# A four-direction scan stage, rebuilt: static slots, turned copies in rings, image-wise merge banks and a product on GpSimd

## What is computed

```python
def _s6(x, xw, xb, bcw, bcb, dw, db, yw, yb):
    u = _linear(x, xw, xb)
    bc = _linear(x, bcw, bcb)
    delta = _linear(x, dw, db)
    Bm, Cm = jnp.split(bc, 2, axis=-1)
    A_bar = jnp.exp(-jax.nn.softplus(delta))
    B_bar = (1.0 - A_bar) * Bm
    elems = (A_bar, B_bar * u)
    ...
    _, h = jax.lax.associative_scan(combine, elems, axis=1)
    y = Cm * h
    return _linear(y, yw, yb)
```

## Time and profile before

| | us |
|---|---|
| median of 3 runs (4073.1 to 4082.28) | 4078.38 |
| the profiled execution, its own time | 4069.57 |
| its span, first to last instruction | 4067.7 |
| from the start of the scan stage's first memset to its end in the trace, about | 2589 to 3295 |
| busy over the whole span: TensorE 83%, VectorE 66%, ScalarE 69%, GpSimd 40% | |

### The profile page before, as it was taken

The page is one execution under the profiler, slowest core; times in us unless marked ns, Lnnn a source line. Parts: engine busy times, 40 slices in busy tenths (PEclk is TensorE's granted clock), DMA queues, the critical chain, the costliest instruction groups (busy, mean ns, idle before and its releaser), DMA issues. The chain is left out here.

```text
span 4067.7 us, 72899 instructions
## 1 busy us (share of the span) xinstructions
PE 3375.5 (83%) x20680; PEld 1903.7 (47%) x20680; DVE 2700.0 (66%) x4346; ACT 2799.4 (69%) x5115; POOL 1643.9 (40%) x1502
## 2 busy tenths in 40 slices
PE   5799999978679899999996668699999868677756
PEld 2688888833234344444442224344444324466622
DVE  2566666667059999999999927466666657322256
ACT  4455555568789889898895439577777659566656
POOL 0233333300258889898897610055555510000000
PEclk9899999989889999999999979899999989889989
DMA  4000000012474665757655122100000012400022
GB/s 94 25 14 14 15 14 15 13 49 53 132 193 129 183 189 150 203 142 201 181 148 141 52 70 59 33 16 15 15 15 15 10 32 59 91 17 13 13 55 52
DMA packets 209772, 297.72 MB, mean 73 GB/s; under 512 B 74150, under 2 KB 194134, under 8 KB 209242
## 3 DMA queue, kind: packets, MB, share of 16 engines
q1 hardware_dynamic: 198826, 285.75, 26.9%
q10 hardware_dynamic: 10800, 10.34, 1.1%
HBM read 193.87 MB, written 102.03 MB: 73 GB/s over the span
## 5 line engine op out<-in xcount | busy, mean ns | idle before, releaser
L1586 POOL TENSOR_TENSOR mam_hc<-mam_h,mam_cs 128x896 f32<-128x896 f32 x336 | 703.8, 2095 | 183.8 <-DVE mam_h L1551 86.0
L1551 DVE TENSOR_TENSOR_SCAN mam_h<-mam_a,mam_kept,mam_dbx 128x448 f32<-128x448 f32 x672 | 738.0, 1128 | 23.5 <-ACT mam_a L1437 22.2
L1318 PE MATMUL mam_ps_y<-mam_hc,mam_ident 128*128 128x448 f32 x1344 | 573.3, 560 | 130.6 <-POOL mam_hc L1586 130.4
L1972 POOL TENSOR_TENSOR scan_ch<-scan_h,scan_cs 128x392 f32<-128x392 f32 x256 | 347.4, 1374 | 554.8 <-DVE scan_h L1938 554.8
L1437 ACT ACTIVATE mam_a<-mam_ft,mam_a_neg 128x448 f32<-128x448 f32 x672 | 409.3, 657 | 79.5 <-DVE mam_h L1551 78.6
L1318 PEld LDWEIGHTS mam_ps_y<-mam_hc,mam_ident 128*128 128x128 f32 x1344 | 250.1, 193 | 431.5 <-POOL mam_hc L1586 219.8
L1538 DVE TENSOR_TENSOR mam_dbx<-mam_ps_u,mam_bs 128x448 f32<-128x448 f32 x672 | 381.3, 611 | 32.3 <-DMA mam_bs<-dram_bc 32.3
L766 POOL TENSOR_TENSOR att_prob<-att_prob,att_share 128x588 f32<-128x588 f32 x128 | 151.8, 1186 | 451.6 <-DVE att_share L951 451.6
L1938 DVE TENSOR_TENSOR_SCAN scan_h<-scan_turned_in,scan_start 128x392 f32<-128x392 f32 x192 | 252.8, 1335 | 27.3 <-ACT scan_turned_in L1857 26.0
L1812 PE MATMUL scan_ps_merged<-scan_ch,scan_w_merge 128*128 128x392 f32 x512 | 231.3, 534 | 45.3 <-POOL scan_ch L1972 43.1
L2092 PE MATMUL lstm_ps<-lstm_hs,lstm_w_h 64*128 64x224 f32 x1344 | 171.1, 409 | 97.9 <-DVE lstm_hs L2175 97.9
(11 more groups left out here) (215 smaller groups left out, 7643.4 us busy)
## 6 DMA issues: line engine op xcount, KB each, us to landing
mam_taps<-normed SPq DMA_DIRECT2D x1008, 43.5 KB
mam_bs<-dram_bc SPq DMA_DIRECT2D x28, 896.0 KB, 14.4
mam_cs<-dram_bc SPq DMA_DIRECT2D x28, 896.0 KB, 16.3
mam_ft<-dram_steps SPq DMA_DIRECT2D x42, 448.0 KB, 4.7
normed<-f_staged SPq DMA_DIRECT2D x384, 38.1 KB
f_mixed<-mixed SPq DMA_DIRECT2D x384, 36.8 KB
dram_gs<-mam_gs SPq DMA_DIRECT2D x56, 224.0 KB, 2.3
mam_gt<-dram_gs SPq DMA_DIRECT2D x56, 224.0 KB, 2.7
```

The source lines that it names most:

```text
L1318: mm = pe.matmul(ps_y[p % 2][:, 0:MT], ident[:], hc[t % 2][:, i, :], start=False, stop=(t % 8 == 7 and i == 1))
L1551: dve.tensor_tensor_scan(h[:, n % 8, :], a[t % 3][:, i, :], dbx[:, i, 0:MT], kept[:, at:at + 1], ALU.mult, ALU.add).then_inc(scanned, 1)
L1586: pool.tensor_tensor(hc[t % 2][:], h[:, row:row + 2, :], cs[:, 2 * pair:2 * pair + 2, :], ALU.mult).then_inc(weighed, 1)
L1972: pool.tensor_tensor(out, hd, in_order(cs, 1 - half, d, t, p), ALU.mult).then_inc(weighed, 1)
```

## The change

The stage is written anew with the same split into slots. A pass of the loop now holds a whole stage of eight slots with fixed addresses. The biases of the four projections come in through w_in: a row of ones is loaded once into a spare partition of each image's input tile. Decay is written twice by ScalarE from its PSUM bank, once by row and once turned into a ring `by_column`; drive is turned once per chunk by one copy. Direction 2 is scanned straight from the rings by row, 1 and 3 from the rings by column. The start values are read from the last column of `h`. The products read PSUM directly: ub = U * rest and drive = B * ub. For every direction TensorE makes one 64-row matmul per image with merged and gate side by side in the image's bank, so ScalarE makes the gate in two parts across the halves, and copies the merged values with their bias into `prod`, also in two parts. GpSimd multiplies `prod` by `gate` in place, after its second `ch` of the slot. `ch`, `gate`, `prod`, `result`, `rest` and `ub` have one buffer each. The diff, cut to its core:

```diff
+        by_column = {name: buf.sbuf(f"{name}_by_column", [P, 2 * PIXELS])
+                     for name in ("decay", "drive")}
-        ps_merged = buf.psum("ps_merged", [P, BANK])
-        ps_gate = buf.psum("ps_gate", [P, BANK])
+        ps_merged = [buf.psum(f"ps_merged{image}", [P, BANK]) for image in range(2)]
...
-                with eng.Fori(0, K // 2 - int(peeled)) as t:
-                    for p in range(2):
-                        slot(f, b, half, t + int(peeled), p, b is not None)
+                first = b is not None and isinstance(b, int) and b == 0
+                for k in range(K):
+                    slot(f, b, half, k, k % 2, b is not None and not (first and k == 0))
...
+                for p in range(2):
+                    for image in range(2):
+                        row = 32 * image + C
+                        sp.dma_start(xin[p][row:row + 1], w["ss_ones"]
+                                     ).then_inc(weights_in, 16)
...
             def _(pe):
-                        pe.wait_ge(sided, done(c - 1, 4))
-                        pe.wait_ge(multiplied, done(c - 1))
-                        for i in range(4):
+                        for i, read, count in (
+                                (DELTA, sided, done(c - 1, 4) - 1), (U, multiplied, done(c - 1)),
+                                (C_, sided, done(c - 1, 4)), (B_, fronted, done(c - 1))):
+                            pe.wait_ge(read, count)
                             pe.matmul(ps_in[i][:, 0:N], w_in[:, i, :], xin[p][:, :, 1:SIDE + 1],
                                       start=True, stop=True).then_inc(projected, 1)
...
-                    pe.wait_ge(gated, done(c - 1))
+                    reached(pe, sigmoided, c)
                     for n in range(DIRS):
                         pe.wait_ge(weighed, done(c - 1, DIRS) + (n + 1))
-                        for a, ps in enumerate((ps_merged, ps_gate)):
-                            mm = pe.matmul(ps[:, 0:N], w_merge[:, a, n, :], ch[p][:, n, :],
+                        for rows, ps in zip((IMAGE_0, IMAGE_1), ps_merged):
+                            mm = pe.matmul(ps[:, 0:N], w_merge[rows, n, :], ch[rows, n, :],
                                            start=(n == 0), stop=(n == DIRS - 1))
...
             def _(act):
                 def open_gate(c, p):
                     act.wait_ge(merged, done(c))
-                    act.wait_ge(gated, done(c - 2))
-                    act.activation(gate[p][:], ps_gate[:, 0:N], ACT.Sigmoid,
-                                   bias=merge_b[:, 1:2]).then_inc(sigmoided, 1)
+                    act.wait_ge(gated, done(c - 1))
+                    act.activation(gate[IMAGE_0], ps_merged[0][IMAGE_1, 0:N], ACT.Sigmoid,
+                                   bias=merge_b[IMAGE_1, 1:2])
+                    act.activation(gate[IMAGE_1], ps_merged[1][IMAGE_0, 0:N], ACT.Sigmoid,
+                                   bias=merge_b[IMAGE_0, 1:2])
+                    act.wait_ge(outed, done(c - 1))
+                    for rows, ps in zip((IMAGE_0, IMAGE_1), ps_merged):
+                        op = act.activation(prod[rows], ps[rows, 0:N], ACT.Identity,
+                                            bias=merge_b[rows, 0:1])
+                    op.then_inc(sigmoided, 1)
+                def turn(c, half, k):
+                    act.wait_ge(fronted, done(c))
+                    act.activation(turned_rows("drive", half, k),
+                                   ring(drive, half)[:, k * N:(k + 1) * N].rearrange(
+                                       "p (y x) -> p y x", x=SIDE), ACT.Copy).then_inc(turned, 1)
+                def slot(f, b, half, k, p, has_tail):
+                    if f is not None and k > 0:
+                        turn(f * K + k - 1, half, k - 1)
+                    elif b is not None and k == 0:
+                        turn(b * K + (K - 1), 1 - half, K - 1)
                     if has_tail:
+                        open_gate(b * K + k - 1, 1 - p)
                     if f is not None:
...
+                        act.wait_ge(multiplied, done(c - 1))
                         act.wait_ge(projected, done(c - 1, 4) + 1)
                         act.activation(ring(decay, half)[:, at], ps_in[DELTA][:, 0:N],
+                                       ACT.Sigmoid, scale=-1.0).then_inc(sided, 1)
+                        act.activation(turned_rows("decay", half, k),
+                                       ps_in[DELTA][:, 0:N].rearrange("p (y x) -> p y x", x=SIDE),
+                                       ACT.Sigmoid, scale=-1.0).then_inc(sided, 1)
+                        act.activation(rest[:], ps_in[DELTA][:, 0:N], ACT.Sigmoid
+                                       ).then_inc(sided, 1)
+                        act.wait_ge(projected, done(c - 1, 4) + 3)
+                        act.activation(ring(cs, half)[:, at], ps_in[C_][:, 0:N], ACT.Copy
+                                       ).then_inc(sided, 1)
+                    if has_tail:
+                        store(b * K + k - 1, 1 - p)
...
             def _(dve):
+                def share(f, k, p):
+                    c = f * K + k
+                    dve.wait_ge(sided, done(c - 1, 4) + 3)
+                    dve.wait_ge(projected, done(c - 1, 4) + 2)
+                    dve.tensor_tensor(ub[:], ps_in[U][:, 0:N], rest[:], ALU.mult
+                                      ).then_inc(multiplied, 1)
+                def drive_with(f, half, k, p):
+                    c = f * K + k
+                    dve.wait_ge(multiplied, done(c))
+                    dve.wait_ge(projected, done(c, 4))
+                    dve.tensor_tensor(ring(drive, half)[:, k * N:(k + 1) * N],
+                                      ps_in[B_][:, 0:N], ub[:], ALU.mult
+                                      ).then_inc(fronted, 1)
...
+                def slot(f, b, half, k, p, has_tail):
                     if b is not None:
+                        c = b * K + k
                         dve.wait_ge(fronted, done(b * K + (K - 1)))
                         dve.wait_ge(scanned, done(c - 1, DIRS))
                         dve.wait_ge(weighed, done(c - 2, DIRS))
+                        for n in range(3):
+                            if n == 2:
+                                dve.wait_ge(turned, done(b * K + (K - 1)))
+                            scan(c, 1 - half, k, p, n)
                     if f is not None:
+                        share(f, k, p)               # ub = ps_in[U] * rest
+                    if b is not None:
+                        scan(c, 1 - half, k, p, 3)
+                    if f is not None:
+                        drive_with(f, half, k, p)    # drive = ps_in[B_] * ub
...
             def _(pool):
+                def tail(c, p):
+                    pool.wait_ge(sigmoided, c + 1)
+                    pool.tensor_tensor(prod[:], prod[:], gate[:], ALU.mult).then_inc(gated, 1)
...
-                    pool.wait_ge(merged, done(c - 2))
+                    pool.wait_ge(merged, done(c - 1))
+                    pool.wait_ge(sided, done(b * K + (K - 1), 4))
                     for n, d in enumerate(ORDER):
...
+                        pool.tensor_tensor(out, hd, in_order(cs, 1 - half, d, k), ALU.mult
                                            ).then_inc(weighed, 1)
+                        if n == 1 and has_tail:
+                            tail(c - 1, 1 - p)
```

More of the change, by code:

```diff
@@ L1717, in stage @@
             def stage(f, b, half):
-                peeled = b is not None and isinstance(b, int) and b == 0
-                if peeled:
-                    for p in range(2):
-                        slot(f, b, half, 0, p, p == 1)
-                with eng.Fori(0, K // 2 - int(peeled)) as t:
-                    for p in range(2):
-                        slot(f, b, half, t + int(peeled), p, b is not None)
+                first = b is not None and isinstance(b, int) and b == 0
+                for k in range(K):
+                    slot(f, b, half, k, k % 2, b is not None and not (first and k == 0))
             stage(0, None, 0)
@@ L1837, in store @@
                         act.dma_start(mixed[c + image * (pairs * K)],
[L1838 removed]
+                                      result[32 * image:32 * image + C]).then_inc(left, 16)
                 def tail(c, p):
                     open_gate(c, p)
[L1842 to L1860 removed]
@@ L1876, in slot @@
-                        act.activation(rest[p][:], ps_in[DELTA][:, 0:N], ACT.Sigmoid,
-                                       bias=biases[:, DELTA:DELTA + 1]).then_inc(sided, 1)
-                        act.wait_ge(projected, done(c, 4))
-                        act.activation(ring(cs, half)[:, at], ps_in[C_][:, 0:N], ACT.Identity,
-                                       bias=biases[:, C_:C_ + 1]).then_inc(sided, 1)
+                                       ACT.Sigmoid, scale=-1.0).then_inc(sided, 1)
@@ L1905, in _, with scan @@
                 dve.wait_ge(prepared, 2)
```

(36 more changed lines are left out.)

153 lines of the change are left out of this document (58 added, 95 removed).

## The result

**3977.35 us** is the median of four runs (3973.53 to 3983.29), against 4075.74 for the kernel before (four runs beside them, 4067.93 to 4082.28): a ratio of 0.9761, with a 95% interval of 0.9738 to 0.9783. The profiled execution took 3975.44 us for its span of 3973.6, the one of before 4069.57 us: 94.1 us less.

The account below looks back on a forecast made before the run. A ring of waits set the old slot; GpSimd's chain with collisions the new, 8.6 us. Full slots -81, last slots -8, front-only -6, start +2.5, tail +2: -90.5 from 4078.38, median 3988 us, forecast 3960 to 4015 (0.66), range 3930 to 4045.

Parts of the forecast that it names:

- TensorE, pairs: Merges of a slot become four pairs whose halves run together: TensorE needs 5.9 us a slot, at worst 8.6.
- rival B: Full slots: pairs don't overlap or strided writes cost 1.84 us; slot 9.3 us, total 4028; 0.13 with C's small form.
- GpSimd's chain: From last merge through four ch and the product to the last pair, with scan collisions: 8.64 us a slot.
- ScalarE's road: From last merge over gate and merged parts, decay, rest, ub, fourth scan and ch to merge: 7.83 us before collisions.
- a fourth ch that waits for a scan that waits for ub by more than 1 us: Sign in a slot that the forecast is wrong and ScalarE's road is the bound.
- The turned copies: ScalarE's turned decay and turned drive, written with a stride: 0.92 us each, bounds 0.48 and 1.84.
- The port: Scans with two SBUF inputs and GpSimd multiplications take turns; ub and drive leave it; no slot under 7.8 us.
- The product's own move: Merged times gate goes from VectorE, 0.60 us away from the port, to GpSimd, 1.02 us on it: a loss.
- Start and front-only slots: Stage start: rows of ones add 2.5 us, 0 to 5; front-only slots 4.3 us each, 6 us less, one table load.
- The last eight slots: Slots without a front keep the GpSimd chain: 8.6 us instead of 9.57, 8 us gained.
- Rival C: TensorE's clock falls to 1.2 GHz in part of the slots as waits grow: slower, 4118 us at share 0.6; chance 0.07.
- Rival A: Scans settle into the holes, so the full slot falls to the port's 7.8 us, total 3937; chance 0.10.

## Why the prediction came out right

The number was right by 11 us, and the slot of 8.6 by 0.16. Point by point:

- **TensorE, pairs.** Right: the two halves of a merge pair start within 0.01 us of each other, and the last pair's four passes take 0.93, where I had 0.82. TensorE's busy time fell by 9 of 80 us. The price of losing them was too small, though: rival B gave 0.66 a slot for pairs that don't overlap, the runs 1.44 and 1.35. The step missed that all eight merges queue behind the output product.
- **The bound of the slot.** GpSimd's chain, which I had at 8.64, measures 8.45. Its terms hold: 0.18 to start for 0.20, the product 0.97 for 1.02, a ch by column 1.20 for 1.21, and the collisions together 0.96 in the first two ch and 0.92 before the fourth, 1.88 for 2.09. What I missed is that ScalarE's road, which I had at 7.83 "before any collision", is 8.45 too. Of the difference, 0.59 is the four parts (2.39 instead of 1.80), 0.51 the collision of the fourth scan, which I had left out of this road, and 0.11 the last merges; against it are decay and turned decay (1.05 instead of 1.40), and 0.24 in small pieces (rest 0.03, ub 0.08, the hand-over to ch 0.12, ch 0.01). The sum is 0.62. I also wrote what would make this road the bound: a fourth ch that waits for a scan that waits for ub by more than 1 us. It came, ub waits 1.75, but what I concluded from it doesn't hold: 1.05 us off that road brought 0.11. The forecast rested on one of two roads that end together, and it was luck that what I had left out of the other didn't push it past.
- **ScalarE.** The turned copies were right: 0.93 and 0.89 each, in the groups of 2740 to 3100 us. The parts were not. I had scaled two parts of 224 columns, 0.90, as if 392 cost the same; they start 0.60 apart. "Biases in w_in cost nothing" was right for TensorE and left a gain out: decay takes 0.50 without a bias, where it took 0.58 with one, and starts the next after 0.39 instead of 0.47. GpSimd's product, 1.01, is as forecast.

```profile
L1966 POOL TENSOR_TENSOR scan_prod<-scan_prod,scan_gate 128x392 f32<-128x392 f32 x43 | 43.3, 1007 | 0.0
...
L1861 ACT ACTIVATE scan_drive_by_column<-scan_drive 128x392 f32<-128x392 f32 x43 | 40.1, 933 | 46.9 <-DVE scan_drive L1939 46.9
...
L1882 ACT ACTIVATE scan_decay_by_column<-scan_ps_in 128x392 f32<-128x392 f32 x43 | 38.2, 889 | 0.0
```

- **The port.** Right: ub and drive, each with one input in PSUM, never grow (minimum, median and longest, ns), while scans of the full slots reach 1.75 us, and one 1.91.

```profile
L1932 DVE TENSOR_TENSOR scan_ub<-scan_ps_in,scan_rest x64: 533/567/568, 2609.2 to 3105.2; 128x392 f32<-128x392 f32 x64
L1939 DVE TENSOR_TENSOR scan_drive<-scan_ps_in,scan_ub x64: 532/533/566, 2609.8 to 3107.1; 128x392 f32<-128x392 f32 x64
```

- **The product's own move** I counted as a loss, and it is one: 0.49 a slot for the engine alone, 0.83 with ScalarE's copies. The Trainium skill (Perfetto Trace Analysis, Optimizing Scalar/DVE Operations) warns of just this, that moving work between VectorE and GpSimd might not help; the run with only the multiplication moved back, 25 us faster, agrees.
- **Start and front-only slots.** The four rows of ones cost nothing: the first projection came at 2604.43 against 2604.40, so +2.5 should have been the lower end, nothing. The front-only slots are 3.59 us each, not 4.3. Their ring is the one that I wrote down, but a turned copy lets the next activation start before it has ended, after 0.73 and 0.65 us and not after 0.92, and decay its turned copy after 0.44. One table load is left, as forecast:

```profile
2606.20 1.28 ACT L1880 ACT_TABLE_LOAD   x1 [20.81 <-PE scan_ps_in L1807]
```

- **The last eight slots.** Wrong in sign. Rival C had the mechanism, a clock that falls as waits grow, but I gave it to the full slots (which kept 1.00) and took the last ones at 8.6. They lost the projections, and with them the clock, 0.65 to 0.67, between the level of 1.2 GHz and that of 2.4. In such a slot the 16 passes of the merges take 5.09 us, and 3.12 with the unread matmuls, the output product 1.57 and 0.87. With 10.32 instead of 8.6 the last seven intervals cost 12 us, what the unread matmuls gave back. The tail ran at the same low clock, 0.67. The Trainium skill (TensorE: Matmul & The Clock Gate, HAM oscillation) describes such throttling of bursts with waits between; the end of this stage agrees, its full slots, at 65 of 80 us busy, don't show it.

Rival A's slot of 7.8, the port's bound, comes in every second slot once rest is made first, but never as a mean with five multiplications on GpSimd. Without the fifth the kernel runs at 7.5 to 7.6. The errors of the pieces, -9, -4, -4, +12 and +2 us, nearly cancelled, and that is luck: the total is better than its steps.

## What to carry to other kernels

Add up every road through a ring, with its collisions, before naming the one that sets the pitch; where two are within a few tenths, shortening one gains almost nothing. A run that removes a wait tells them apart only if the wait didn't come back as another, so read its timeline before its time. Splitting a matmul's rows so that halves run together was worth 1.35 to 1.44 us a slot here, because it also shortened what queues behind a waiting matmul, while handing GpSimd a multiplication that VectorE can do from PSUM cost 0.83, ScalarE's two copies included. And look at the slots where a pipeline empties: there the clock can fall though the steady ones keep it.

## What was not expected of the hardware

- Work that nobody reads made the kernel 12 us faster, by the clock alone (0.67 to 0.97, 10.32 to 8.73 a slot).
- A 64-lane activation of 392 columns takes 0.58 us and starts the next after 0.60. Of 128 lanes and the same columns, with a bias as well, the kernel before's decay takes 0.58 and starts the next after 0.47; without a bias the changed kernel's takes 0.50 and starts the next after 0.39. So half the lanes saved nothing. Why the parts start further apart I didn't try.
- A strided write costs the activation as much as a strided read did, 0.93 and 0.89, but the one from PSUM lets the next start after 0.66.
- At the head of the loop with 16 unrolled slots ScalarE stood 3.64 us for issue, twice in the stage, which makes slots of 11.5 and 11.2. The five kernels whose product reads PSUM on VectorE all have it, also the one with 128-row merges at 8.96 a slot (3.70 and 3.59 us, slots of 10.08 and 9.88). No other kernel made here has it, not even the one that multiplies the copies on VectorE, at 7.95. What it is made of stays open.
